# Fourth layer of a graph network: float32 scatter products against three bfloat16 parts

## The reference, cut to what matters

```
def _L3_gnn_ref(feat, weight, loop_weight, norm, src, dst, etypes):
    all_h = jnp.einsum('ni,rio->rno', feat, weight)     # 8 relations
    msg = all_h[etypes, src] * norm                     # 200000 x 128
    h = jax.ops.segment_sum(msg, dst, num_segments=feat.shape[0])
    h = h + feat @ loop_weight
    return h
...
h = jnp.maximum(_layernorm(x, axis=-1), 0.0)
x = x + _L3_gnn_ref(h, L3_gnn_weight, L3_gnn_loop_weight, edge_weight1, src, dst, edge_type_8)
```

## Time and profile before

| | |
|---|---|
| median of 3 runs | 6484.98 us (6475.8 to 6511.51) |
| the profiled execution's own time | 6506.78 us |
| its span in the trace | 6505.0 us |
| mean granted TensorE clock, as a share of 2.4 GHz | 0.757 |
| PE / PE weight loads / DVE / ACT / POOL busy, share of the span | 59% / 45% / 44% / 21% / 61% |
| gathers of the fourth layer, first and last start | 4464.2 to 6481.2 us |
| dense way of the fourth layer, last eviction | 5918.9 us |
| the chain that ended last: PE / another core or an unknown queue / DVE / issue | 30% / 29% / 18% / 15% |

### The profile page before, as it was taken

The page is one execution under the profiler, slowest core; times in us unless marked ns, Lnnn a source line. Parts: engine busy times, 40 slices in busy tenths (PEclk is TensorE's granted clock), DMA queues, the critical chain, the costliest instruction groups (busy, mean ns, idle before and its releaser), DMA issues.

```text
span 6505.0 us, 67690 instructions
## 1 busy us (share of the span) xinstructions
PE 3841.2 (59%) x20041; PEld 2943.2 (45%) x20041; DVE 2889.6 (44%) x9205; ACT 1395.3 (21%) x5456; POOL 3944.1 (61%) x4092
## 2 busy tenths in 40 slices
PE   3666666755555555555565478885555656555333
PEld 2333334454544445455554356652444444444322
DVE  6655544465555555556655523333333222222222
ACT  3222222233333333333333301122000000000000
POOL 0556666546666666666666466643666666666665
PEclk7677878777677777777777699997777777776666
DMA  3233333354545455554545455554111111111121
GB/s 96 80 98 103 115 104 116 99 146 144 156 141 161 142 156 148 154 146 142 162 142 155 131 176 191 193 178 151 47 46 47 46 46 47 46 47 46 47 61 46
DMA packets 317033, 731.21 MB, mean 112 GB/s; under 512 B 76720, under 2 KB 157644, under 8 KB 304380
## 3 DMA queue, kind: packets, MB, share of 16 engines
q0 software_dynamic: 172432, 405.32, 23.0%
q1 hardware_dynamic: 142220, 320.61, 14.5%
q10 hardware_dynamic: 2016, 0.92, 0.1%
HBM read 598.71 MB, written 127.83 MB: 112 GB/s over the span
## 4 chain that ended last, share of the span: by engine, by line
PE 30%; another core or an unknown queue 29%; DVE 18%; issue 15%; ACT 4%; DMA 2%; DVEq 1%; POOL 1%; SPq 1%; ACTq 0%; POOLq 0%
PE ps L2187 9%; DVE oneh L1601 5%; PE ps L2143 4%; PE ps L2172 3%; PE ps L2150 3%; DVE ps L1707 2%; DMA third<-dst_flat 2%; PE ps L2104 2%; PE ps L2114 2%; ACT turned_words L1431 2%; PE ps L2210 1%; PE ps L2056 1%; DVE third L1699 1%; DVE turned_words L1664 1%
## 5 line engine op out<-in xcount | busy, mean ns | idle before, releaser
L1261 POOL DMA_INDIRECT rows<-tab_rel,third x1415 | 1356.8, 959 | 775.3 <-issue 517.4
L1261 POOL DMA_INDIRECT rows<-tab_h,idx_src x1086 | 1059.9, 976 | 822.9 <-issue 356.6
L1261 POOL DMA_INDIRECT rows<-tab_hp,idx_src x1120 | 1075.6, 960 | 603.0 <-issue 300.0
L2143 PE MATMUL ps<-oneh,rows 128*128 128x128 f32 x2830 | 527.8, 338 | 698.9 <-issue 344.5
L2210 PE MATMUL ps<-third 128*128 128x128 f32 x3126 | 597.7, 350 | 485.1 <-issue 266.1
L2143 PEld LDWEIGHTS ps<-oneh,rows 128*128 128x128 f32 x2830 | 470.0, 244 | 786.0 <-issue 416.8
L2210 PEld LDWEIGHTS ps<-third 128*128 128x128 f32 x3126 | 531.4, 255 | 580.8 <-issue 334.9
L2187 PE MATMUL ps<-third,h 128*120 128x384 bf16 (+17 forms) x3773 | 712.2, 340 | 19.8 <-ACT h L1390 10.3
L1431 ACT ACTIVATE turned_words<-turned_words 128x128 f32<-128x128 f32 x1563 | 463.1, 300 | 693.0 <-DVE turned_words L1712 558.5
L2187 PEld LDWEIGHTS ps<-third,h 128*120 128x120 bf16 (+10 forms) x3773 | 494.3, 134 | 185.1 <-issue 21.2
L1261 POOL DMA_INDIRECT third<-tab_hp,idx_src x443 | 425.7, 961 | 224.0 <-issue 119.2
(11 more groups left out here) (247 smaller groups left out, 5470.9 us busy)
## 6 DMA issues: line engine op xcount, KB each, us to landing
third<-dst_flat SPq DMA_DIRECT2D x390, 256.0 KB
h<-cnt_d SPq DMA_DIRECT2D x48, 1568.0 KB
cnt_d<-h SPq DMA_DIRECT2D x29, 1568.0 KB
cnt_d<-third SPq DMA_DIRECT2D x19, 1568.0 KB
tab_rel<-rows SPq DMA_DIRECT2D x49, 512.0 KB, 2.6
rows<-tab_rel,third POOLq DMA_INDIRECT x1415
rows<-tab_hp,idx_src POOLq DMA_INDIRECT x1120
rows<-tab_h,idx_src POOLq DMA_INDIRECT x1086
```

Of the source, the lines that this page charges most:

```text
L1261: pool.indirect_dma_start(out=to[:, t, 0:n], out_offset=None, in_=table[:, :], in_offset=bass.IndirectOffsetOnAxis(ap=idx[:, col:col + 1], ...
L2143: last = pe.matmul(far3_banks[v % 3][:, 0:P], rows[:, slot, t, :], oneh[:, g % NONE_F, t, :], start=start, stop=stop)
```

## The change

The fourth layer's gathered part is rebuilt after the third's. The rows have 5 slots in place of 10 (`R3_SLOT`), and 5 new slots (`PART_SLOT`, three in what the rows gave up, two in `third`) hold each group's three bfloat16 parts. For each group ACT multiplies the four gathered tiles by the edge weights in place (four activations), and copies them as bfloat16 to the high part; DVE subtracts it from the rows; one turn later ACT copies the rest to the middle part and DVE writes the difference to the low part. The row slot is free once DVE has done that (`s_wlow`). The one-hots are plain bfloat16, four buffers; PE does one product of 384 columns per tile, a turn later than before, and bundles end by `finish_far` as in the third layer, in two banks in place of three. `out3`, of the dense way, moves from `gsum` to `tmp_words`. Cut to its core:

```diff
-        rows_at = [rows[:, k, :, :] for k in range(NSLOT)]
+        rows_at = [rows[:, k, :, :] for k in range(R3_SLOT)]
...
-            slots = (H3_SLOT, HP_SLOT, H3_SLOT, NSLOT)[layer]
+            slots = (H3_SLOT, HP_SLOT, H3_SLOT, R3_SLOT)[layer]
...
-                plan.append(("onehot", dict(layer=layer, g=g, scat=n_scat.get(g - (NONE if layer in (0, 2) else NONE_F), 0),
+                plan.append(("onehot", dict(layer=layer, g=g, scat=n_scat.get(g - (NONE_F if layer == 1 else NONE), 0),
...
-                slot_free[g % slots] = (s_scat, n_scat[g])
+                if layer != 3:
+                    slot_free[g % slots] = (s_scat, n_scat[g])
...
-                    far_tails[v] = (finish3 if layer == 3 else finish_far)(v, n_scat[g])
+                    far_tails[v] = finish_far(v, n_scat[g])
...
+            def weigh(g):
+
+                n_weigh[g] = dict(g=g, slot=g % slots, part=g % PART_SLOT, row=n_row[g], scat=n_scat.get(g - PART_SLOT, 0),
+                                  weighed=s_wrow.up(), high=s_whigh.up(), rest=s_wrest.up(), mid=s_wmidp.up(), low=s_wlow.up())
+                slot_free[g % slots] = (s_wlow, n_weigh[g]["low"])
+                plan.append(("weigh", n_weigh[g]))
+
+            def finish_parts(g):
+                plan.append(("parts", n_weigh[g]))
...
+            elif layer == 3:
+                steps = ((0, gather), (0, onehot), (1, finish_parts), (0, weigh), (1, scatter))
             else:
-                steps = ((0, gather), (0, onehot), (0 if layer == 3 else 1, scatter))
+                steps = ((0, gather), (0, onehot), (1, scatter))
...
+                elif kind == "weigh":
+                    g, v, parts = st["g"], rows_at[st["slot"]], parts3[st["part"]]
+                    m = tiles[g]
+                    act.wait_ge(s_row[st["slot"]].handle, st["row"])
+                    for t in range(m):
+                        col = g * TPG + t
+                        last = act.activation(v[:, t, :], v[:, t, :], ACT.Copy, scale=wt[:, col:col + 1])
+                    last.then_inc(s_wrow.handle, 1)
+                    act.wait_ge(s_wrow.handle, st["weighed"])
+                    if st["scat"]:
+                        act.wait_ge(s_scat.handle, st["scat"])
+                    act.copy(parts[:, 0:m, 0:P], v[:, 0:m, :]).then_inc(s_whigh.handle, 1)
+                elif kind == "parts":
+                    m, parts = tiles[st["g"]], parts3[st["part"]]
+                    act.wait_ge(s_wrest.handle, st["rest"])
+                    act.copy(parts[:, 0:m, P:2 * P], rows_at[st["slot"]][:, 0:m, :]).then_inc(s_wmidp.handle, 1)
...
+                elif kind == "weigh":
+                    m, parts = tiles[st["g"]], parts3[st["part"]]
+                    v = rows_at[st["slot"]][:, 0:m, :]
+                    dve.wait_ge(s_whigh.handle, st["high"])
+                    dve.tensor_tensor(out=v, in0=v, in1=parts[:, 0:m, 0:P], op=ALU.subtract).then_inc(s_wrest.handle, 1)
+                elif kind == "parts":
+                    m, parts = tiles[st["g"]], parts3[st["part"]]
+                    v = rows_at[st["slot"]][:, 0:m, :]
+                    dve.wait_ge(s_wrest.handle, st["rest"])
+                    dve.wait_ge(s_wmidp.handle, st["mid"])
+                    dve.tensor_tensor(out=parts[:, 0:m, 2 * P:3 * P], in0=v, in1=parts[:, 0:m, P:2 * P], op=ALU.subtract
+                                      ).then_inc(s_wlow.handle, 1)
...
-                    pe.wait_ge(s_row[slot].handle, st["row"])
+                    if st["layer"] == 3:
+                        pe.wait_ge(s_wlow.handle, st["low"])
+                    else:
+                        pe.wait_ge(s_row[slot].handle, st["row"])
...
                         if st["layer"] == 3:
-                            last = pe.matmul(far3_banks[v % 3][:, 0:P], rows[:, slot, t, :], oneh[:, g % NONE_F, t, :],
+                            last = pe.matmul(far_banks[v % 2][:, 0:3 * P], onehb[:, g % NONE, t, :], parts3[g % PART_SLOT][:, t, :],
                                              start=start, stop=stop)
```

More of the change, by code:

```diff
@@ L695, in scatter @@
                 n_scat[g] = s_scat.up()
-                slot_free[g % slots] = (s_scat, n_scat[g])
+                if layer != 3:
+                    slot_free[g % slots] = (s_scat, n_scat[g])
                 first, last = g == g_bundles[v][0], g == g_bundles[v][-1]
-                banks = 3 if layer == 3 else 2
                 if first:
-                    for _ in far_tails.pop(v - banks, ()):
+                    for _ in far_tails.pop(v - 2, ()):
                         pass
                 plan.append(("scatter", dict(layer=layer, g=g, v=v, slot=g % slots, sums=sums, one=n_one[g], row=n_row[g],
-                                             first=first, last=last, add=n_gadd.get(v - banks, 0))))
+                                             first=first, last=last, add=n_gadd.get(v - 2, 0),
+                                             low=n_weigh[g]["low"] if layer == 3 else 0)))
                 if last:
-                    far_tails[v] = (finish3 if layer == 3 else finish_far)(v, n_scat[g])
+                    far_tails[v] = finish_far(v, n_scat[g])
                     tails.append(far_tails[v])
+            n_weigh = {}
+            def weigh(g):
[5 more added lines that the diff above has]
+                plan.append(("parts", n_weigh[g]))
             def finish_far(v, scat):
@@ L1596, in vector_program @@
                         dve.wait_ge(s_gate.handle, st["gate"])
-                    if st["layer"] in (1, 3):
+                    if st["layer"] == 1:
                         for t in range(m):
                             col = g * TPG + t
-                            by = gate[:, g % 2, t:t + 1] if st["layer"] == 1 else wt[:, col:col + 1]
-                            last = dve.tensor_scalar(oneh[:, g % NONE_F, t, :], iota_b[:, :], dst_rel[:, col:col + 1], by,
-                                                     ALU.is_equal, ALU.mult)
+                            last = dve.tensor_scalar(oneh[:, g % NONE_F, t, :], iota_b[:, :], dst_rel[:, col:col + 1],
+                                                     gate[:, g % 2, t:t + 1], ALU.is_equal, ALU.mult)
                         last.then_inc(s_one.handle, 1)
@@ L1649, in vector_program @@
                     dve.tensor_tensor(out=a, in0=a, in1=v, op=ALU.add).then_inc(s_add.handle, 1)
-                elif kind == "far3_add":
-                    u = len(bundles) + st["v"]
-                    dve.wait_ge(s_scat.handle, st["scat"])
-                    if st["add"]:
-                        dve.wait_ge(s_add.handle, st["add"])
-                    start = dve.value_load(base_bint[0:1, u:u + 1], min_val=0, max_val=npad - P)
-                    a = acc[:, 0, bass.ds(start, P)]
-                    dve.tensor_tensor(out=a, in0=a, in1=far3_banks[st["v"] % 3][:, 0:P], op=ALU.add).then_inc(s_add.handle, 1)
+                elif kind == "weigh":
[10 more added lines that the diff above has]
+                                      ).then_inc(s_wlow.handle, 1)
                 elif kind == "pair":
```

21 lines of the change are left out of this document (14 added, 7 removed).

## The result

The changed kernel takes 6559.19 us (median of 10 runs, 6522.91 to 6590.54), the kernel before on the same chip 6485.76 us (10 runs, 6475.16 to 6511.51). The ratio is 1.0107, with a 95% interval of 1.0083 to 1.0131: 73 us slower, where 56 were forecast. The profiled execution of after took 6540.25 us by its own time and 6538.4 by its span. Its first three layers happen to end 32.7 us earlier than those of the profiled execution before (the fourth layer's first gather starts at 4431.50 in place of 4464.2), so the two profiles are compared from that gather on. From the first gather's start to the last one's it was 2017.0 us; now it is 6521.70 - 4431.50 = 2090.2, **73 us more**. The loss lies in the stretch where I looked for it, but not in the row in which I looked for it.

The account below looks back on a forecast made before the run. The prediction took POOL's gather pace in the fourth layer as the bound; 0 + 0 + 0 + 50 (slots) + 6 (tail) = +56 us on the median of 6484.98 gave 6541 us, range 6390 to 6670.

Parts of the forecast that it names:

- What bounds the kernel: Fourth layer's gathered part: POOL sets the pace; its 257.9 us of waits are all PE, DVE or ACT can win.
- PE: Fourth layer's products: 198 us less from products, 25 us added for bundle turns, hidden beside POOL's issue; worth 0.
- DVE against POOL: Fourth layer's gathers: float32 one-hots that fall away cost POOL nothing visible; gathers keep 0.95 us; taken as 0.
- DVE's own time: Fourth layer: one-hots, subtractions and additions give DVE 355 us more, at most 47% busy, hidden behind POOL.
- ACT: Fourth layer: activations, casts and copies take 870 to 1120 us, 43 to 56% of the stage; enough room by itself.
- The slots: Fourth layer's row slots: PE may be late by 6 to 8 groups, not 10; POOL waits 50 us more.
- The tail: After the last gather lands: added activations, casts and subtractions lengthen the end by 6 us (0 to 15).
- The waits go: Fourth layer: PE keeps up, POOL waits less; 6362 us with half the waits gone, 6233 with all; chance 0.27.
- ACT becomes a link: Fourth layer: ACT's queue serialises with PE's, wait per gather 0.303 us or more; 6662 us; chance 0.15.

Follow-up runs that it names:

- sets 2 and 3: Second and third groups of follow-up runs, each beside the kernel before on the same chip; that kernel's medians there were 5657.79 and 5661.57 us.
- e6: Kernel before, with 5 row slots in the fourth layer in place of 10; ratio 0.9998, 5661.57 us for the kernel before beside it not implied.
- e3: Kernel before, with two added DVE tensor_tensor subtractions of 128x512 float32, both inputs in SBUF, per fourth-layer group; ratio 1.0144.
- e4: Kernel before, with two added DVE tensor_scalar subtractions of a constant, 128x512 float32, one SBUF input, per fourth-layer group; ratio 1.0058.
- e11: Changed kernel, weighted rows in PSUM for both subtractions, row slot free after the activations, plain one-hots as four tensor_scalar of 128x128; 5655.14 us, ratio 0.999.
- e9: Changed kernel, unaltered, measured again beside the kernel before; 5787.59 us, ratio 1.0232.
- e1: Changed kernel, weighted rows held in one PSUM bank, so both subtractions read PSUM; 6690.61 us, ratio 1.0225.
- e2: Changed kernel, weighted rows in one PSUM bank for both subtractions, and row slot free after the four activations; 6737.07 us, ratio 1.0304.
- e7: Changed kernel, only the first subtraction reads weighted rows from PSUM, the rest goes back to the row slot; ratio 1.0159.
- e10: Changed kernel, each 128x512 subtraction made as four of 128x128; ratio 1.0133.
- e5: Changed kernel, both subtractions replaced by tensor_scalar over the same 128x512 elements, one SBUF input; ratio 1.0126.
- set 1: First group of follow-up runs, beside the kernel before on the same chip; that kernel's median there was 6544.65 us.

## Why the prediction was right in its sum and wrong in its terms

The time that was forecast for the median was 6541 us, and 6559.19 was measured; +56 was forecast and +73 measured. That the sum came near is luck, as the terms show.

- **What bounds the kernel.** That POOL's pace is the thing to reckon, and that a wait of POOL is all that PE, DVE and ACT can win, was right, and I gave 1.24 us per gather as the floor. In sets 2 and 3 the kernel before runs at it (1784.6 / 1414 = 1.26 in e6). What I missed is that others can also lengthen POOL's own instruction.
- **PE.** 170 us less busy was forecast. The product took 0.281 us ((237.7 + 160.4) / 1415) and not 0.233, at the lower clock that I had named; so 398.1 us against 527.8, and with 36.3 us for the turns' passes 93 us less. Its worth of 0 stands at the second pace, where POOL never waits for it (e6). At the first pace no run isolates it.
- **DVE against POOL: this is the step that failed.** I took 0, "POOL's gathers of this layer keep 0.95 us". They took 1.046. I had looked only at the one-hots that fall away, which are four short instructions, and not at what the three long ones that come do to a gather. The effect, though not its size, was there to be read in the trace before: the dense way's DVE instruction of 128x784 (L1618, about 0.69 us) was there in the stretch with 0.966 us (351.62 / 364) and gone in that with 0.942, and I put the difference down to "the stretch beside the dense way" without asking which row of it. In that trace the 78 gathers that begin inside L1618 take 1082 ns in the mean, and the 1010 that begin beside an idle DVE 946. Nor did the one-hots that fall away cost quite nothing: the 272 gathers that begin in one of them take 974 ns, some 8 us over all. Of the page of the Trainium skill that I cited I used the sentence that a tensor_tensor leaves the descriptors' write side free. The same list says that one with two inputs in SBUF contends with a GpSimd instruction that reads SBUF. The gather reads its indices from an SBUF tile (`third`, in its row), and the runs went by that sentence (e3: 1134 ns in place of 959).
- **DVE's own time.** 355 us more were forecast; DVE's total went from 2889.6 to 3232.5, 343 more. ACT: 870 to 1120 us were forecast, 863 measured (2258.1 - 1395.3), with 392 ns per activation, between my 300 and 482.
- **The slots.** The term was +50 us of waits, to about 310 and more often; they fell to 196.8, in 58 waits in place of 93. That DVE's second subtraction would release them was right. Part of that fall has a simple cause: POOL, slower by itself, reaches a late slot later. By the exchange of e3 and e4, 0.24 to 0.37 us of time for each us of longer gathers, the 123.6 us are 30 to 46 of the 73 us. The other 27 to 43 are an estimate of what the slots, ACT's place in the chain or the one turn's delay cost at the first pace. My 50 may be these, but no run isolates them, and this stays open. At the second pace the term is nothing (e6, e11).
- **The tail.** 6 us were forecast. At the first pace the time from the last gather's start to the end went the other way in the two profiles, from 6505.0 - 6481.2 = 23.8 us to 6538.4 - 6521.7 = 16.7. Where PE is on time, it is 5786.2 - 5769.3 = 16.9 us in e9 and 5657.8 - 5645.9 = 11.9 in e6: 5 us more.
- **The rivals.** "The waits go" had the right sign for the waits and the wrong one for the time. Its argument that late completions hold POOL for 2.6 us at most in the third layer left out the other row, with 7.8. "ACT becomes a link" is what e1 and e2 turned into at the first pace, by a bank of mine and not by the change. None of the rivals had the gathers' own length in it. With 124 us as the upper bound of the term that I set to 0, such a rival would have stood at +130 us, which is 6615 here and too much. In set 3, where POOL doesn't wait, 126 was measured, and it would have been nearer than my +56.

So the forecast of +56 us met +73 by luck: the 50 us put on waits stand where 124 us on the gathers less 61 us of waits belong. At the pace of e9 the same working would have been off by more than half: 126 us.

## What to carry to other kernels

Where one engine's own instructions set the pace, ask of each added instruction not only whether its time is hidden beside that engine, but whether it lengthens that engine's instructions. The rows that tell are the mean of one instruction in stretches with and without the suspect. For gathers issued by POOL, DVE instructions should be short, or take their inputs from PSUM: here one of 0.69 us per group of four gathers costs each gather about 34 ns (e9 less e7: 1046 - 1012; two back to back cost 175 together, e3: 1134 - 959), four of 0.29 us in its place about 15 (e9 less e10 is 39 ns for two, so 19 or 20 less for each). A buffer added to cure this (the one PSUM bank) must not tie a stage to the end of the stage behind it; and a loss measured where the pace-setter often waits is smaller than the loss where it never does.

## What the runs showed that I had not expected

- **A gather is held by a DVE instruction, and DVE's source decides.** Gathers get longer with DVE work on 128x512 from SBUF, be it tensor_tensor (0.69 us, 1134 ns in e3) or tensor_scalar (0.43 us, 1068 ns in e4; 0.55 us, 1005 ns in e5). They are hardly held if the same tensor_tensor has one input in PSUM (e1: 973 and 946 ns, e11: 960 and 944, for those that begin inside one). ACT's casts and activations hold nothing: the gathers of e11 have all of them beside them and take 957 ns. The Trainium skill ("SBUF — State Buffer", Who interferes with whom) infers that a tensor_tensor spares the making of descriptors; here no such sparing is seen, since tensor_tensor alone lengthens the gathers by 247 us in e3.
- **One kernel has two paces.** The kernel before took 6485.76 us beside after and 6544.65 in set 1, but 5657.79 and 5661.57 us in sets 2 and 3, 13% less. The difference lies in POOL's waits: in the second layer 358.3 us before, and in e6, which is the same kernel in that layer, only steps of 0.3 us:

```profile
POOL rows L1261 <- issue: 313.2, 1028, 0.3
POOL third L1261 <- issue: 125.8, 413, 0.3
POOL rows L1261 <- PE ps L2146: 2.4, 8, 0.3
POOL third L1261 <- PE ps L2146: 0.9, 3, 0.3
```

  The granted clock in the fourth layer's first 520 us is 0.84 in e6 and 0.73 in the earlier trace rows, but the products are equally long (210 and 212 ns), so PE is not slower in its passes, it pauses between them. What makes it pause in two measurements and not in the two others wasn't found, nor whether it goes with the chip or with the time of the run. At the slow pace the chain through the one PSUM bank is paid for (e2: 1.0304), at the quick one it isn't (e11, which has the same chain: 0.999), and with longer gathers it is the other way about: 1.0107 for the change at the one, 1.0232 at the other.
